# One column tile of the second half's g sums issued before TensorE's wait for the second part of h, in an LSTM scan on one core

## What is computed

```
a = x_t @ Wx + b + prev_h @ Wh
i, f, o = sigmoid(a[:, :H]), sigmoid(a[:, H:2H]), sigmoid(a[:, 2H:3H]);  g = tanh(a[:, 3H:])
next_c = f * prev_c + i * g
next_h = o * tanh(next_c)
...
x = x + lstm(x, cond_1024, Wx, Wh, b)
x = x + ((x * ys) @ weight) * d          # ys, d follow from cond_1024 and weight
```

## Time and profile before

| | us |
|---|---|
| median of 3 runs | 1782.44 (1782.10 to 1782.82) |
| the profiled execution, device time | 1781.28 |
| its span, first to last instruction | 1779.5 |
| PE busy / PEld busy | 1674.8 (94%) / 1618.9 (91%) |
| ACT busy / DVE busy / POOL busy | 1096.3 (62%) / 1001.7 (56%) / 259.7 (15%) |
| mean granted TensorE clock, share of full speed | 0.993 |

### The profile page before, as it was taken

One profiled execution on the slowest core, in us unless ns is written; L12 is line 12 of the kernel. 1 busy time (PEld: TensorE's weight loads), 2 busy tenths in 40 slices (PEclk: granted clock), 3 DMA queues, 4 the chain that ended last, 5 costly groups with the idle time before them and its releaser, 6 DMA issues.

```text
span 1779.5 us, 356718 instructions
## 1 busy us (share of the span) xinstructions
PE 1674.8 (94%) x164620; PEld 1618.9 (91%) x164620; DVE 1001.7 (56%) x7455; ACT 1096.3 (62%) x8196; POOL 259.7 (15%) x1293
## 2 busy tenths in 40 slices
PE   7999999999999999999999999999999999999998
PEld 6999999999999999999999999999999999999996
DVE  2555555555555555555555555555555555555554
ACT  2666666666666666666666666666666666666663
POOL 0111111111111111111111111111111111111110
PEclk7999999999999999999999999999999999999999
DMA  2000000000000000000000000000000000000001
GB/s 78 26 0 0 0 0 0 0 0 0 0 0 0 0 0 0 0 0 0 0 0 0 0 0 0 0 0 0 0 0 0 0 0 0 0 0 0 0 0 47
DMA packets 4585, 6.69 MB, mean 4 GB/s; under 512 B 1248, under 2 KB 3040, under 8 KB 4576
## 3 DMA queue, kind: packets, MB, share of 16 engines
q1 hardware_dynamic: 3872, 5.51, 0.9%
q10 hardware_dynamic: 704, 1.05, 0.2%
HBM read 4.46 MB, written 2.10 MB: 4 GB/s over the span
## 4 chain that ended last, share of the span: by engine, by line
PE 82%; DVE 12%; ACT 3%; issue 2%; DMA 0%; SPq 0%; POOL 0%; DVEq 0%
PE pG L228 32%; PE pX L210 18%; PE pH L228 14%; PE pS L228 14%; DVE pH L373 4%; DVE pH L349 4%; PE pF L241 3%; ACT fgate L186 3%; DVE hst L380 2%; DVE parts L368 2%; DVE pG L345 1%; PE pG L310 1%; DMA xh<-in_xT_dram 0%; PE pS L301 0%; DVE ores L397 0%
## 5 line engine op out<-in xcount | busy, mean ns | idle before, releaser
L228 PE MATMUL pG<-hst,wh_sb 128*32 128x16 f32 x65536 | 1081.6, 187 | 89.0 <-DVE hst L380 87.8
L228 PEld LDWEIGHTS pG<-hst,wh_sb 128*32 128x32 f32 x65536 | 943.4, 109 | 136.9 <-DVE hst L380 112.6
L186 ACT ACTIVATE fgate<-pH 128x2 f32<-128x2 f32 x2048 | 353.9, 173 | 601.0 <-PE pH L228 600.6
L228 PE MATMUL pH<-hst,wh_sb 128*32 128x16 f32 x32768 | 673.4, 185 | 3.5 <-issue 3.5
L368 DVE TENSOR_TENSOR parts<-fgate,pH 128x2 f32<-128x2 f32 x2048 | 320.3, 156 | 583.6 <-ACT fgate L186 583.4
L228 PEld LDWEIGHTS pH<-hst,wh_sb 128*32 128x32 f32 x32768 | 589.0, 110 | 2.1 <-issue 2.1
L228 PE MATMUL pS<-hst,wh_sb 128*32 128x16 f32 x32768 | 506.8, 186 | 3.4 <-issue 3.4
L210 PE MATMUL pX<-xp,wx_sb 128*32 128x8 f32 x32896 | 459.6, 181 | 2.9 <-issue 1.8
L228 PEld LDWEIGHTS pS<-hst,wh_sb 128*32 128x32 f32 x32768 | 424.4, 108 | 3.6 <-issue 3.6
L147 POOL TENSOR_TENSOR xh<-xh,hst 128x4 f32 (+1 forms) x1024 | 208.7, 204 | 1490.3 <-DVE hst L380 1490.3
L373 DVE TENSOR_TENSOR_SCAN pH<-parts 128x6 f32<-128x6 f32 x2048 | 367.2, 179 | 82.9 <-ACT parts L188 0.9
(11 more groups left out here) (41 smaller groups left out, 179.4 us busy)
## 6 DMA issues: line engine op xcount, KB each, us to landing
outT_dram<-ores SPq DMA_DIRECT2D x8, 256.0 KB, 2.5
xh<-in_xT_dram SPq DMA_DIRECT2D x6, 320.0 KB
wh_sb<-in_Wh_dram ACTq DMA_DIRECT2D x1, 1024.0 KB, 7.9
wx_sb<-in_Wx_dram SPq DMA_DIRECT2D x1, 1024.0 KB, 7.4
w_sb<-in_w_dram SPq DMA_DIRECT2D x1, 256.0 KB, 6.2
xh<-in_xT_dram SPq DMA_DIRECT2D x2, 64.0 KB, 8.0
condT<-in_condT_dram ACTq DMA_DIRECT2D x1, 2.0 KB, 7.6
bias_col<-in_bC_dram ACTq DMA_DIRECT2D x1, 3.0 KB, 7.3
```

The costliest lines, as they stand in the source:

```text
L186: act.activation(fgate[:, j, :], forgets[j][:, cols], ACT.Sigmoid).then_inc(fgate_ready[j], 1)
L228: last = pe.matmul(to[c * Q:(c + 1) * Q, :], tile(wh_sb[:, k, :], c, j, g), hst[:, k, WIDE * t:WIDE * (t + 1)], start=False, stop=True, sk ...
```

## The change

One call of `cell` is split in two. The tile of strip 0 of the cell "half 1, g gate, part 0 of h" is issued right after half 1's i cell, ahead of the wait for h1; the tiles of strips 1, 2 and 3 of that cell stay where the whole cell was. Nothing is added or removed.

```
--- before.py
+++ after.py
@@ -266,6 +266,7 @@
                     if s == 0:
                         pe.wait_ge(pair_carried, it + 1)
                     cell(s, 1, 0, 0)
+                    cell(s, 1, 2, 0, (0,))
 
                     pe.wait_ge(h_ready[1], it * T + (s + 1))
                     cell(s, 0, 1, 1).then_inc(fsum_ready[0], 1)
@@ -273,7 +274,7 @@
                     cell(s, 0, 2, 1).then_inc(sums_ready[0], 1)
                     cell(s, 1, 1, 0)
                     cell(s, 1, 1, 1).then_inc(fsum_ready[1], 1)
-                    cell(s, 1, 2, 0)
+                    cell(s, 1, 2, 0, range(1, G))
                     cell(s, 1, 0, 1)
                     cell(s, 1, 2, 1).then_inc(sums_ready[1], 1)
                     if s == 0:
```

## The result

| | before | changed |
|---|---|---|
| median, us | 1782.56 (4 runs, 1782.10 to 1782.82) | 1819.32 (4 runs, 1816.95 to 1820.82) |
| ratio, 95% interval | | 1.0206 (1.0193 to 1.0219) |
| span of the profiled execution, us | 1779.5 | 1815.2 |
| mean granted clock, share of full speed | 0.993 | 0.994 |

The change costs 36.8 us, 0.036 us in each of 1024 steps. The median step of the trace grew from 1.692 to 1.726 us, which makes 34.8 us. The profiled execution's span grew by 35.7: the first step of each body now takes 1.728, and a few irregular steps differ. The last 1.1 us of the 36.8 are spread between executions, for the profiled one was the fastest of the changed kernel's four.

A forecast was written before the change was run, and what follows sets the result against it. The h0-to-h0 ring of 1.692 us a step was taken to bound the kernel. Four parts cost 0; the strip order cost 0.045 us a step, 46 us over 1024 steps, giving 1828 us, range 1779 to 1842, likeliest case 1810 to 1842.

The forecast's parts named there:

- The ring and the wait: h0, 14 cells on TensorE, o sigmoid, h0: 1.692 us a step; the wait for h1 ends just in time, some 0.01.
- (a): One tile, 0.017 us, goes ahead of the wait; still 14 cells between h0 and the o sums: cost 0.
- (c): The wait for h1 may end 0.017 later without harm, taken up in a body's last step: cost 0.
- (d): Waits for `pair_carried` and `xp_ready`, the queues of DVE, ACT, POOL and SP, and all signals keep their place: cost 0.
- Part (b): Half 0's f and g sums come 0.017 later; tanh stays 0.07 ahead of the o sigmoid, cover 0.02 us: cost 0.
- Part (e): Strip 0 gets two tiles in succession, the second 0.060 behind the first, not 0.017: 0.045 a step, 46 us; chance 0.48.
- few ns for the round that skips strip 0: Small addition to the 0.043 lost by the second tile, for the later round without strip 0, making 0.045 a step.
- If tiles overtake: Strips 1 to 3 overtake, stream does not stop; tanh pushes the o sigmoid by 0.02 to 0.045, 25 to 45 us.
- The estimate of 34 us: About 60 cycles overhead a matmul, 25 ns a record on a strip; 2 x 25 - 17 = 33 ns a step.
- No change: Rival: the limit of 0.017 a tile is common to all strips; 1782.4, give or take 3; chance 0.29.
- Faster: Rival: the 0.04 gap in weight loads at the wait is lost time the tile fills; 17 us gained, 1765; chance 0.11.
- A small loss: Rival: a strip is held half a round only, second tile one place late; 17 us, 1800; chance 0.12.

The follow-up runs named there:

- experiment 1: Changed kernel with the five cells behind the wait for h1 taking their strips in the order 1, 2, 3, 0; ratio 1.000 to the kernel before.
- the probe: Kernel before plus ten blocks of 48 matmuls on zeros at the start; 0.032 us a record on one strip with 16 columns, 0.016 on two.
- strips 3, 2 and 1: Three runs: changed kernel with that strip's tile, not strip 0's, moved ahead of the wait; ratios 1.0056, 1.0097 and 1.0141.
- 8: Kernel before with half 1's f cell on h1 in strip order 3, 0, 1, 2, a repeat late in the stream; ratio 0.9997.
- 9: Changed kernel with only the first cell behind the wait (half 0's f cell on h1) in strip order 1, 2, 3, 0; ratio 1.0047.
- 5: Kernel before, no tile moved, half 1's i cell on h0 in strip order 1, 2, 3, 0, repeating strip 0 across the wait; ratio 1.0012.
- 6: Kernel before with half 0's f cell on h0 in strip order 1, 2, 3, 0, strip 0 repeated one cell earlier; ratio 0.9993.
- 4: Kernel before, nothing moved, half 0's i cell on h1 in strip order 3, 0, 1, 2, repeating strip 3; ratio 1.0030.

## Why the prediction was right, and where its size was off

- **The ring and the wait.** The step was held by h0, 14 cells and the o sigmoid, and the wait for h1 ended just in time. This held: with the tile moved and nothing lost (experiment 1) the step is 1692 ns as before. Steps of the changed kernel in which h1 came 195 to 197 ns after h0, not 266, have the f sigmoid at 692 to 694 all the same.
- **Parts (a), (c), (d), at no cost.** Shown by experiment 1 for the three together. There h1 comes 10 ns later at the end of a body (274 and not 264 ns after h0), as (c) foresaw, and the next step takes 1692 all the same.
- **Part (b), the cover of 0.02.** For the one tile the cost of nothing held, but barely. The distance to the tanh shrank from 89 to 79 ns, and 79 is the least that is free: the cover was 10 ns and the tile used all of it. That is luck in the size, for the prediction took 0.07 as enough from the earlier trace rows, where the o sigmoid lasts 0.17 and not 0.16. For two tiles it did not hold: 9 ns foreseen, 19 measured, and 42 foreseen, 52 measured for four. The statement that failed is "all beyond them is paid once for once".
- **Part (e), the strips.** The forecast rested on strips being nearly full, with the second tile 0.060 behind the first. The strip's pace was right: 32 ns a record, two make 63. The size was too large: 0.045 foreseen, 0.034 to 0.036 measured, 46 us against 36.8. The mis-sized term is the loss given the distance: I subtracted one place, 63 - 17 = 46, as if every later tile waited. In fact tiles of other strips overtake, the signalled record of the first cell behind the wait starts on time, and only its signal is late, by 34 and not by 46. How the other 12 ns are absorbed is not shown. The "few ns for the round that skips strip 0" are 0: from the first f sigmoid to half 1's i and g sigmoid the difference falls by one tile, 50 to 34, as counted.
- **If tiles overtake.** The prediction had this as the other branch of the same case, with the stream not held up and half 0's chain alone late. The tiles do overtake, and yet the stream is late, half 1's sums too. Both branches described a part. The tanh did not push the o sigmoid, as this branch had it: it starts 79 ns ahead of it, and the o sigmoid lasts 158 ns.
- **The estimate of 34 us.** By the Trainium skill, "TensorEngine Tiling (Array Packing)", Instruction Overhead, the prediction worked out an estimate of 34 us. The sum came nearer to the result than mine by luck: its time for a record, 25 ns, is below the 32 measured on one strip at full clock, and it too subtracts only one place; the two errors nearly cancel.
- **The rivals.** "No change" fell by the result: its claim that only a common pace counts is refuted by the probe (0.032 a record on one strip, 0.016 on two). "Faster" fell by experiment 1: the gap of 0.04 in the weight loads was no loss. "A small loss" needed a record of 17 ns on a strip, and the probe has 32; losses near its size, 8, 14 and 24 ns, came with strips 3, 2 and 1, for another reason.

What stays open is how TensorE absorbs a lag, and why the signal is late when its own record is not. The rule that fits best (records 32 ns apart on a strip, sums out in program order, some 42 ns allowed) foresaw experiments 8 and 9 to 1 ns, missed strip 2 by 5, and expected 8 and 12 ns in experiments 5 and 6, where 0 to 1 were lost. In those two the strip's earlier tile came three places later than usual, so that the strip had been free and this tile may have started early; that is argued and not shown. Shown are only these: order of strips alone decides (1), a repeat is free or nearly so where strips were only permuted (4, 5, 6, 8: 0 to 6 ns, and 12 in the first steps of bodies in 5), and an additional tile on one strip ahead of the first signal, with the cells behind it in their old order, costs 8 to 34 ns, more the sooner that strip is needed again. With one of these cells turned it costs 7, with all of them turned nothing.

## What to carry to other kernels

Where narrow tiles run side by side in column strips and the strips are nearly full, look at the order of the tiles around one that you move: the same move cost 2% with strip 0 twice in succession and nothing with the cells behind it turned by one. A wait that ends just as the stream reaches it needs no filling; look for steps of the trace in which it ended earlier, and see whether anything came sooner. Time lost by order inside the matmul stream shows as busy time, so measure the distance from the input to the first instruction that reads each sum.

## What the runs showed of the hardware

- A strip of 32 columns of weights took one float32 matmul record in 32 ns with 16 moving columns at full clock. At half clock 8, 16 and 32 columns took 0.054 us alike. With 64 columns at full clock a record took 0.058. Four strips ran side by side.
- Matmul records of a later cell start ahead of one that is held up by its strip (963.85 before 963.87). A record that starts at its usual place (425 ns) can have its signal 34 ns late (671 and not 637) when another strip lags.
- A signal adds about 25 ns to the stream: two cells and a signal take 159 ns, three and a signal 226.
- The o sigmoid on ACT, close behind the tanh, ended 236 to 237 ns behind the tanh's start: it lasted 168 ns at a distance of 68, 160 at 76, and 157 from 79 on.
